# A 12-stage perceiver kernel on one core: weights of three late stages loaded two stages earlier, and a new order of TensorE's work between the scores of the rotary attention

## The chip, the cores and the metric

The kernel runs on one core of a Trainium2 chip. The metric is the device time of one execution in microseconds (us); lower is better. All values are float32.

## The reference

A residual `x` (16 batches of 64 latents, 128 features) goes through four layers of three blocks. Each block reads the layer-normed residual and adds its result to it. The last six are the ones that matter here:

```python
x = x + L2_xattn(ln(x), ctx, ctx, ...)   # single-head attention to 1601 context rows a batch
x = x + L2_attn(ln(x), ...)              # x+g1*(ln(x)@proj_w.T+proj_b), then an MLP of width 512
x = x + L2_ffn(ln(x), ...)               # mixture of 8 experts, the best 2
x = x + L3_xattn(ctx, ln(x), ...)        # 8 heads of 64, context keys with rotary positions
x = x + L3_attn(ln(x), ...)              # 16 heads of 8, latent attention:
    q_lat = (x @ Wq_down).reshape(b, t, 16, 64)
    q_c, q_e = q_lat @ Wq_up_c, q_lat @ Wq_up_e       # k in the same way, v = v_lat @ Wv_up
x = x + L3_ffn(ln(x), ...)               # gated recurrence over 32 steps:
    f = sigmoid(x_t @ wf.T + c @ uf.T + bf)           # i and g in the same way, with wi, ui, wc, uc
    c = f * c + i * g
```

## The kernel before, in words

The residual stays in SBUF as `lat` [128, 8, 128]. The 12 blocks are 12 stages, one after the other. A stage owns its SBUF and PSUM tensors and its semaphores; each has a program for every engine (SP issues all DMAs, PE, ACT, DVE, POOL), written out by hand, and its order is that of the code. When a stage ends, its semaphores are cleared and all engines meet at a barrier (L51 to L54). So no work of one stage lies beside another's, and each stage begins by loading its weights.

**L2_xattn** (`single_head_stage`, L1726). Work goes by pairs of batches. SP loads the context of a pair into `staged` (L1799 to L1803) when the pair before has left it; PE turns (transposes) it (L1867), makes the scores (L1879), turns the probabilities (L1890) and sums (L1903). Pairs 0, 1 and 2 are issued first, the rest in a loop.

**L2_attn** (`projected_mlp_stage`, L3006). SP issues 14 loads: three weights (`proj_rows`, `fc1_rows`, `fc2_rows`, 576 KB) and eleven small ones. PE waits for all of them (L3056), turns the weights in nine transposes (L3059 to L3062), turns the first half of the normalised tokens `z` (L2503) and multiplies by the projection (L3067). DVE makes the second `z` out of it, PE turns that too, and then come the matmuls of fc1 (L3076). ACT takes the square roots of both layer norms (L148), copies the turned weights out of PSUM (L3102 to L3104) and then the turned `z` (L2516).

**L3_xattn** (`rotary_attention_stage`, L1076). 16 batches (8 pairs, parity 0 and 1), each with four tiles t = 0 to 3 of two heads each, so 64 tiles. For a tile PE makes the scores of two heads against 1665 keys (L1290, eight matmuls of 512 columns and two short ones), ACT the exponentials and their scaling by the row sums (L1479). Behind the scores follow four slots j = 0 to 3. In each, PE turns a quarter of the probabilities of the tile before (`turn_probs`, L1302; the last slot has two short transposes), makes a quarter of the next tile's keys (`project`, L1278 to L1280), does one or two tiles of the sums (L1316) and, in some slots (`BETWEEN`, L1102), a "between": in t = 1 and 2 it turns four tiles of the next batch's context (L1258) at j = 1 and 2 (1) or j = 1 and 2 (2); in t = 0 of odd batches it makes the next pair's queries at j = 1 (L1265); in t = 3 of even ones the output at j = 2. `turn_probs` and the between share one PSUM bank, `bank_a`, which ACT must empty into SBUF before PE fills it again: L1486 for the probabilities, L1451 for the context, L1457 for the queries, which L1461 then places with four copies. The keys go on over DVE (L1665, L1667) and POOL (L1600), which makes `projected`, the input of the next scores.

**L3_attn** (`latent_attention_stage`, L3186). SP issues three loads of 512 KB (`down`), ten of 1 to 2 KB (`up`) and five more. PE turns `down` in 24 transposes (L3266), multiplies it by `up` (L3274, 24 products of 24 or 16 columns), so that up and down projection are folded into `heads` and `headsV`, turns the normalised residual `y` (L2503), and multiplies (L3284). `y` comes from DVE (L139).

**L3_ffn** (`gated_recurrence_stage`, L3479). SP issues eight loads of 64 KB (`rows`, the gate weights) and five small ones (`bias`). PE waits for all 13, turns the eight weights (L3523), turns `y` (L2503) and multiplies (L3535); 16 steps follow one after the other.

## Time and profile before

| | |
|---|---|
| median of 3 runs | 2897.18 us (2894.28 to 2900.27) |
| the profiled execution, its own time | 2901.51 us |
| its span in the trace | 2899.4 us |
| busy: PE, DVE, ACT, POOL | 2575.8, 1792.9, 1632.2, 1403.3 us |
| mean granted TensorE clock | 0.93 of full speed |
| L2_xattn, from about 1628 to 1754 | 126 us |
| L2_attn, to 1817 | 63 us |
| L3_xattn with its start, 1945 to 2722 | 777 us |
| L3_attn, to 2832 | 110 us |
| L3_ffn, to 2899 | 67 us |

The profiled execution took 4.33 us longer than the median. Times in the trace count from the start of the span. Busy PE time is the time in which matmuls are under way, not work at full rate.

### The profile page before, as it was taken

How to read it: one execution, taken by the hardware profiler on the slowest of the kernel's cores; microseconds unless marked ns; L12 is line 12 of the kernel's file. 1: busy time of each engine (PE TensorE's matmuls, PEld its weight loads, DVE VectorE, ACT ScalarE, POOL GpSimd, SP SyncE). 2: the span in 40 equal slices, each digit the busy share in tenths (PEclk: the TensorE clock that was granted, in tenths of full speed). 3: DMA queues.
4: the chain of work that ended last, by engine and by line, in shares of the span. 5: the costliest groups of instructions: out<-in, count | busy, mean ns of one | idle time of the engine just before them, and what ended most of it. 6: DMA issues, size and time to landing. Idle time of an engine off the chain costs nothing. (4 is left out here: it accounts for less than half of the span.)

```text
span 2899.4 us, 43919 instructions
## 1 busy us (share of the span) xinstructions
PE 2575.8 (89%) x16307; PEld 2149.0 (74%) x16307; DVE 1792.9 (62%) x3737; ACT 1632.2 (56%) x2861; POOL 1403.3 (48%) x1112
## 2 busy tenths in 40 slices
PE   5999998687999999999958795878999999999767
PEld 4899988476999999999957564775666676666546
DVE  7888874545555555545535446437888888888262
ACT  4888884335666666666623343325666666665332
POOL 1787774112666666666600260206566665665040
PEclk9999999788999999999978897888999999999775
DMA  3323321013111111110001240211000000000000
GB/s 109 104 75 99 105 59 36 14 30 87 35 35 35 35 29 41 29 42 24 12 8 42 72 114 16 59 32 58 13 24 13 24 21 16 24 13 1 25 1 15
DMA packets 222574, 117.83 MB, mean 41 GB/s; under 512 B 21368, under 2 KB 217632, under 8 KB 222368
## 3 DMA queue, kind: packets, MB, share of 16 engines
q1 hardware_dynamic: 222368, 115.11, 14.4%
q8 instruction: 127, 2.08, 0.3%
q14 instruction: 79, 0.65, 0.1%
HBM read 100.39 MB, written 13.64 MB: 39 GB/s over the span
## 5 line engine op out<-in xcount | busy, mean ns | idle before, releaser
L846 POOL TENSOR_TENSOR L_xattn_held<-L_xattn_held,L_xattn_shift 128x512 f32<-128x512 f32 (+1 forms) x613 | 762.8, 1290 | 296.5 <-ACT L_xattn_shift L766 296.4
L564 PEld LDWEIGHTS L_xattn_acc<-L_xattn_rows,L_xattn_held 128*128 128x128 f32 (+2 forms) x5120 | 618.4, 192 | 34.8 <-DVE L_xattn_mixed L949 9.2
L564 PE MATMUL L_xattn_acc<-L_xattn_rows,L_xattn_held 128*128 128x129 f32 (+2 forms) x5120 | 627.9, 275 | 5.6 <-DVE L_xattn_mixed L949 5.6
L970 DVE TENSOR_TENSOR L_xattn_running<-L_xattn_ring,L_xattn_running 128x512 f32<-128x512 f32 (+1 forms) x384 | 264.2, 688 | 268.7 <-PE L_xattn_ring L546 257.0
L1600 POOL TENSOR_TENSOR L_xattn_projected<-L_xattn_along,L_xattn_crossed 128x512 f32<-128x512 f32 (+1 forms) x256 | 271.6, 1072 | 280.9 <-DVE L_xattn_crossed L1667 279.1
L756 ACT ACTIVATE L_xattn_held<-L_xattn_held 128x512 f32<-128x512 f32 (+2 forms) x640 | 400.4, 631 | 0.2
L749 ACT COPY L_xattn_held<-L_xattn_ring 128x512 f32<-128x512 f32 (+1 forms) x416 | 243.3, 585 | 227.9 <-DVE L_xattn_running L970 193.3
L544 PE MATMUL L_xattn_ring<-L_xattn_queries_hi,L_xattn_keys_hi 128*128 128x512 f32 (+2 forms) x640 | 281.7, 440 | 3.4 <-DVE L_xattn_keys_lo L874 2.0
L546 PE MATMUL L_xattn_ring<-L_xattn_queries_hi,L_xattn_keys_lo 128*128 128x512 f32 (+2 forms) x640 | 254.0, 397 | 0.0
L545 PE MATMUL L_xattn_ring<-L_xattn_queries_lo,L_xattn_keys_hi 128*128 128x512 f32 (+2 forms) x640 | 253.6, 396 | 0.0
L1316 PE MATMUL L_xattn_sums<-L_xattn_probT,L_xattn_rows 128*128 128x256 f32 (+2 forms) x896 | 249.7, 386 | 0.6 <-ACT L_xattn_mixed L1492 0.6
L1486 ACT COPY L_xattn_probT<-L_xattn_bank_a 128x512 f32<-128x512 f32 (+2 forms) x320 | 138.9, 454 | 175.3 <-PE L_xattn_bank_a L1302 173.9
L1290 PE MATMUL L_xattn_score<-L_xattn_projected,L_xattn_queries 128*128 128x512 f32 (+1 forms) x512 | 199.6, 526 | 8.8 <-POOL L_xattn_projected L1600 8.3
L747 ACT ACTIVATE L_xattn_held<-L_xattn_ring,L_xattn_mask_now 128x512 f32<-128x512 f32 (+1 forms) x224 | 153.3, 684 | 74.8 <-DVE L_xattn_running L966 59.3
L1665 DVE TENSOR_TENSOR L_xattn_along<-L_xattn_bank_p,L_xattn_rot_cos 128x512 f32<-128x512 f32 (+1 forms) x256 | 151.6, 592 | 49.5 <-PE L_xattn_bank_p L1280 45.2
L1290 PEld LDWEIGHTS L_xattn_score<-L_xattn_projected,L_xattn_queries 128*128 128x128 f32 x512 | 95.7, 193 | 115.1 <-issue 56.5
L1316 PEld LDWEIGHTS L_xattn_sums<-L_xattn_probT,L_xattn_rows 128*128 128x128 f32 (+2 forms) x896 | 160.8, 192 | 24.8 <-issue 0.9
L966 DVE SCALAR_TENSOR_TENSOR L_xattn_running<-L_xattn_ring,L_xattn_mask_now,L_xattn_running 128x512 f32<-128x512 f32 (+2 forms) x208 | 154.6, 743 | 29.1 <-PE L_xattn_ring L546 26.2
L1302 PE MATMUL L_xattn_bank_a<-all_ident,L_xattn_prob 128*128 128x128 f32 (+2 forms) x896 | 145.4, 279 | 29.2 <-ACT L_xattn_turned L1451 14.9
L1675 DVE TENSOR_REDUCE L_xattn_peak<-L_xattn_score 128x1 f32<-128x1024 f32 (+1 forms) x128 | 127.1, 1021 | 64.6 <-PE L_xattn_score L1290 63.3
L1302 PEld LDWEIGHTS L_xattn_bank_a<-all_ident,L_xattn_prob 128*128 128x128 f32 (+2 forms) x896 | 103.0, 142 | 72.4 <-ACT L_xattn_turned L1451 36.8
L1667 DVE TENSOR_TENSOR L_xattn_crossed<-L_xattn_bank_p,L_xattn_rot_sin 64x512 f32<-64x512 f32 (+1 forms) x256 | 152.1, 594 | 3.5
(575 smaller groups left out, 4866.6 us busy)
## 6 DMA issues: line engine op xcount, KB each, us to landing
L_xattn_raw<-in_ctx SPq DMA_DIRECT2D x16, 768.0 KB
context_normalised<-L_xattn_fresh SPq DMA_DIRECT2D x16, 768.0 KB
L_xattn_rows<-context_normalised SPq DMA_DIRECT2D x16, 768.0 KB
L_xattn_fresh<-in_ctx SPq DMA_DIRECT2D x16, 768.0 KB
L_xattn_rows<-in_ctx SPq DMA_DIRECT2D x16, 768.0 KB
L_xattn_staged<-in_ctx SPq DMA_DIRECT2D x16, 768.0 KB
L_xattn_xhat<-context_normalised SPq DMA_DIRECT2D x16, 768.0 KB
L_ffn_w<-in_L_ffn_W SPq DMA_DIRECT2D x2, 896.0 KB, 5.4
```

The lines of the kernel that those rows point to most:

```text
L544: nc.tensor.matmul(bank, hi, q_hi, start=True, stop=False)
L545: nc.tensor.matmul(bank, hi, q_lo, start=False, stop=False)
L546: nc.tensor.matmul(bank, lo, q_hi, start=False, stop=True).then_inc(tile_done, 1)
L564: mm = nc.tensor.matmul(acc[:, c // 2, c % 2 * WIDE:(c % 2 + 1) * WIDE], held[0:n, u % 2, k, c * P:(c + 1) * P], rows[0:n, b % 2, k, :], s ...
L749: kept = nc.scalar.copy(dst, bank)
L756: nc.scalar.activation(held[0:n, u % 2, k, :], held[0:n, u % 2, k, :], ACT.Exp, scale=scale).then_inc(prob_ready, 1)
L846: nc.gpsimd.tensor_tensor(tile, tile, shift[0:keys_of_tile[k]], ALU.subtract).then_inc(shifted, 1)
L970: seen = nc.vector.tensor_tensor(most, bank, most, ALU.max)
L1290: mm = nc.tensor.matmul(score[:, c0:c0 + n], queries[:, pair % 2, parity, t * P:(t + 1) * P], projected[:, t % 2, c0:c0 + n], start=True, ...
L1302: turn = nc.tensor.transpose(bank[0:n, i * P:(i + 1) * P], prob[:, t % 2, c0:c0 + n], core.ident[:])
L1316: mm = nc.tensor.matmul(sums[:, 0:GCOLS], rows[0:n, parity, k, :], probT[0:n, group, k, :], start=(k == 0), stop=(k == KT - 1))
L1600: nc.gpsimd.tensor_tensor(projected[:, t % 2, c0:c0 + n], along[:, c0:c0 + n], crossed[:, c0:c0 + n], ALU.add)\
```

## The change

1. A new class `Ahead` holds `heads`, `headsV` and `gate_wT` in SBUF until the program ends, and the rows of the weights while L2_xattn and L2_attn run. Its 24 loads (3 for the MLP, 3 `down`, 8 gate weights, 10 `up`; some 2.6 MB) are issued on SP in L2_xattn, behind the loads of pair 2 and ahead of those of pair 3. The MLP has 11 loads left, L3_attn 5 and L3_ffn 5. POOL's memset of `up` goes along.
2. In L2_attn PE waits for the three weights alone, turns them, then turns `down` (24 transposes) and the gate weights (8) through three banks, and makes the 24 products `heads` between the projection and the turn of the second `z`. ACT has the eight copies `keep_later` between its square roots, and the copies of `heads`. DVE has the four small operations on `up`.
3. L3_attn and L3_ffn lose these loads, transposes, copies and products.
4. In the rotary attention the sums lie in a slot according to `SPLIT`, and in the slot behind one with a between `project` comes ahead of `turn_probs`. On ACT the copies that place the queries and the rounding of the own keys move from the slot of the between to the next one, behind its copy of the probabilities.
5. There is one more clearing of semaphores with its barrier behind L2_attn, and one more at the program's end.

```diff
+    SPLIT = {0: ((2, 0), (1, 1), (2, 0), (1, 0)), 1: ((2, 0), (1, 1), (2, 0), (1, 0)),
+             2: ((2, 0), (1, 1), (2, 0), (1, 0)), 3: ((2, 0), (2, 0), (1, 1), (1, 0))}
...
+                        if projects and j - 1 in BETWEEN[t]:
+                            project(*following(pair, parity, t), j)
                         if turns:
                             turn_probs(*preceding(pair, parity, t), j)
-                        if projects:
+                        if projects and j - 1 not in BETWEEN[t]:
                             project(*following(pair, parity, t), j)
...
                         if turns:
                             keep_probs(preceding(pair, parity, t)[2], j)
+                        if BETWEEN[t].get(j - 1) == "queries" and not last:
+                            if parity == 1:
+                                place_queries(pair + 1)
+                            keep_own(*after)
...
             load_staged(1, 1)
             during(0, 0)
+            core.ahead.load(sp, weights(core.w, "L2_attn"), weights(core.w, "L3_attn"), weights(core.w, "L3_ffn"))
             with sp.Fori(0, (PAIRS - 2) // 2 - 1) as j:
...
+            pe.wait_ge(ahead.down_loaded, ahead.DOWN_LOADS)
+            pe.wait_ge(ahead.gate_loaded, ahead.GATE_LOADS)
+            for n, (kind, j) in enumerate(LATER):
+                if n >= 3:
+                    pe.wait_ge(later_kept, n - 2)
...
             turn_tiles_pe(nc, pe, core.ident[:], z[:], bank[0:2], z_ready, 1, z_turned, by_halves=True)
...
+        with ExitStack() as loading:
+            core.ahead = Ahead(nc, ctx, loading)
+            STAGES["L2_xattn"](core, w)
+            STAGES["L2_attn"](core, w)
```

PE in the rotary attention, a tile t = 1, from the first turn of context (L1258, after L1261) at j = 1 to the last slot. `prob` are the probabilities, `bank_p` the keys. Before:

```order
L1258 MATMUL L_xattn_bank_a<-all_ident,L_xattn_gained 128x128 x4
L1316 MATMUL L_xattn_sums<-L_xattn_probT,L_xattn_rows 128x256
L1302 MATMUL L_xattn_bank_a<-all_ident,L_xattn_prob 128x128 x4
L1278 MATMUL L_xattn_bank_p<-L_xattn_keys_hi,L_xattn_wk_hi 128x512
L1279 MATMUL L_xattn_bank_p<-L_xattn_keys_hi,L_xattn_wk_lo 128x512
L1280 MATMUL L_xattn_bank_p<-L_xattn_keys_lo,L_xattn_wk_hi 128x512
L1316 MATMUL L_xattn_sums<-L_xattn_probT,L_xattn_rows 128x256
L1258 MATMUL L_xattn_bank_a<-all_ident,L_xattn_gained 128x128 x4
L1316 MATMUL L_xattn_sums<-L_xattn_probT,L_xattn_rows 128x256
L1302 MATMUL L_xattn_bank_a<-all_ident,L_xattn_prob 65x128
```

And now:

```order
L1261 MATMUL L_xattn_bank_a<-all_ident,L_xattn_gained 128x128 x4
L1319 MATMUL L_xattn_sums<-L_xattn_probT,L_xattn_rows 128x256
L1281 MATMUL L_xattn_bank_p<-L_xattn_keys_hi,L_xattn_wk_hi 128x512
L1282 MATMUL L_xattn_bank_p<-L_xattn_keys_hi,L_xattn_wk_lo 128x512
L1283 MATMUL L_xattn_bank_p<-L_xattn_keys_lo,L_xattn_wk_hi 128x512
L1305 MATMUL L_xattn_bank_a<-all_ident,L_xattn_prob 128x128 x4
L1319 MATMUL L_xattn_sums<-L_xattn_probT,L_xattn_rows 128x256 x2
L1261 MATMUL L_xattn_bank_a<-all_ident,L_xattn_gained 128x128 x4
L1281 MATMUL L_xattn_bank_p<-L_xattn_keys_hi,L_xattn_wk_hi 128x130
L1282 MATMUL L_xattn_bank_p<-L_xattn_keys_hi,L_xattn_wk_lo 128x130
L1283 MATMUL L_xattn_bank_p<-L_xattn_keys_lo,L_xattn_wk_hi 128x130
L1305 MATMUL L_xattn_bank_a<-all_ident,L_xattn_prob 65x128
```

Between a turn of context and the turn of probabilities behind it there now lie one matmul of the sums and three of the keys (first place), or the three short ones of the keys and no sums (second place).

ACT in the rotary attention, a tile t = 0 of an odd batch, from the queries' bank on. Before:

```order
L1457 COPY L_xattn_asked<-L_xattn_bank_a 128x512
L1461 COPY L_xattn_queries<-L_xattn_asked 32x8x64 x4
L1442 CAST L_xattn_keys_hi<-L_xattn_yT 128x64
L1486 COPY L_xattn_probT<-L_xattn_bank_a 128x4x128
L1486 COPY L_xattn_probT<-L_xattn_bank_a 65x128
```

And now:

```order
L1463 COPY L_xattn_asked<-L_xattn_bank_a 128x512
L1495 COPY L_xattn_probT<-L_xattn_bank_a 128x4x128
L1470 COPY L_xattn_queries<-L_xattn_asked 32x8x64 x4
L1449 CAST L_xattn_keys_hi<-L_xattn_yT 128x64
L1495 COPY L_xattn_probT<-L_xattn_bank_a 65x128
```

The copy of the probabilities of slot 2 goes ahead of the four copies that place the queries.

ACT at the start of L2_attn. Before:

```order
L148 ACT_TABLE_LOAD
L148 ACTIVATE L_attn_stats<-L_attn_square,all_small 128x4 x4
L3102 COPY L_attn_fc1T<-L_attn_bank 128x512
L3103 COPY L_attn_fc2T<-L_attn_bank 128x512
L3104 COPY L_attn_projT<-L_attn_bank 128x128
L2516 ACTIVATE L_attn_zT<-L_attn_bank,L_attn_cols 128x512 x2
```

And now:

```order
L3144 COPY L_attn_projT<-L_attn_bank 128x128
L3145 COPY L_attn_fc1T<-L_attn_bank 128x512
L148 ACT_TABLE_LOAD
L148 ACTIVATE L_attn_stats<-L_attn_square,all_small 128x4 x2
L3147 COPY L_attn_fc2T<-L_attn_bank 128x512
L3141 COPY L_attn_downT<-L_attn_bank 128x512 x4
L148 ACTIVATE L_attn_stats<-L_attn_square,all_small 128x4 x2
L3141 COPY L_attn_downT<-L_attn_bank 128x512 x2
L3141 COPY ahead_gate_wT<-L_attn_bank 128x512 x2
L2530 ACTIVATE L_attn_zT<-L_attn_bank,L_attn_cols 128x512 x2
```

Two copies stand ahead of the first square root, and nine between it and the turned `z`.

## Rows read from the trace of the kernel before

**Rows 1.** Windows: the rotary loop, 4 us of L2_xattn, 4 us of L3_attn.

```profile
core 0: us, PE busy (x) PEld busy (x) DVE busy (x) ACT busy (x) POOL busy (x), PEclk, DMA share, GB/s
1990.00:2700.00 710.00, 673.54 (x3329) 484.58 (x3327) 582.22 (x989) 451.61 (x721) 429.81 (x351) 1.00 0.06 17
1656.00:1660.00 4.00, 4.00 (x19) 3.46 (x18) 0.92 (x2) 1.42 (x3) 1.44 (x1) 0.50 1.06 288
2732.00:2736.00 4.00, 3.04 (x21) 2.37 (x20) 0.47 (x4) 2.25 (x4) 0.00 (x0) 0.87 0.20 44
```

**Rows 2.** Timeline of L3_attn's start: start, us, engine, [idle before <- releaser].

```profile
2722.83 0.36 SPq L3243 DMA_DIRECT2D L_attn_down<-in_L_attn_Wq_down  x1
2727.16 1.11 DVE L139 TENSOR_SCALAR L_attn_y<-all_lat,L_attn_square,L_attn_stats 128x128 f32<-128x128 f32 x4
2729.37 4.25 PE L3266 MATMUL L_attn_bank<-all_ident,L_attn_down 128*128 128x128 f32 x20 [8.72 <-DMA L_attn_down<-in_L_attn_Wv_down]
2730.80 0.59 SPq L3251 DMA_DIRECT2D L_attn_wc<-in_L_attn_Wc  x1
2735.23 9.30 PE L3274 MATMUL L_attn_bank<-L_attn_up,L_attn_downT 128*128 128x24 f32 x48 [0.77 <-ACT L_attn_downT L3366]
2746.99 5.20 PE L3284 MATMUL L_attn_bank<-L_attn_heads,L_attn_yT 128*128 128x384 f32 x10 [0.68 <-ACT L_attn_yT L2514]
```

**Rows 3.** Timeline of L3_ffn's start.

```profile
2836.03 0.43 SPq L3517 DMA_DIRECT2D L_ffn_bias<-in_L_ffn_bf  x1
2836.54 1.11 DVE L139 TENSOR_SCALAR L_ffn_y<-all_lat,L_ffn_square,L_ffn_stats 128x128 f32<-128x128 f32 x4
2840.04 1.97 PE L3523 MATMUL L_ffn_bank<-all_ident,L_ffn_rows 128*128 128x128 f32 x8 [9.90 <-DMA L_ffn_bias<-in_L_ffn_in_c]
2844.49 2.79 PE L3535 MATMUL L_ffn_bank<-L_ffn_yT,L_ffn_wT 128*128 128x64 f32 x12 [0.77 <-ACT L_ffn_yT L2514]
```

**Rows 4.** Waits of the rotary stage (us idle, times, longest); then its timeline, a tile t = 1.

```profile
PEld L_xattn_bank_a L1302 <- ACT L_xattn_turned L1451: 36.8, 60, 1.0
...
2356.76 0.66 PE L1302 MATMUL L_xattn_bank_a<-all_ident,L_xattn_prob 128*128 128x128 f32 x4 [0.30 <-ACT L_xattn_turned L1451]
2357.17 0.48 PE L1278 MATMUL L_xattn_bank_p<-L_xattn_keys_hi,L_xattn_wk_hi 128*128 128x512 f32 x1
2360.75 2.96 PE L1290 MATMUL L_xattn_score<-L_xattn_projected,L_xattn_queries 128*128 128x512 f32 x8
```

**Rows 5.** Timeline: a tile t = 0 of an odd batch, from the queries' copies.

```profile
2391.87 2.50 ACT L1461 COPY L_xattn_queries<-L_xattn_asked 32x512 f32<-32x512 f32 x4
2395.18 0.43 PE L1302 MATMUL L_xattn_bank_a<-all_ident,L_xattn_prob 128*65 128x128 f32 x2 [1.12 <-ACT L_xattn_probT L1486]
2396.22 1.02 PE L1290 MATMUL L_xattn_score<-L_xattn_projected,L_xattn_queries 128*128 128x512 f32 x2
```

**Rows 6.** Timeline of L2_xattn: SP's loads and PE's turns of pair 3.

```profile
1655.95 2.86 SPq L1803 DMA_DIRECT2D L_xattn_staged<-in_ctx  x1
1666.43 0.40 SPq L1801 DMA_DIRECT2D L_xattn_staged<-in_ctx  x1
1676.45 1.09 PE L1867 MATMUL L_xattn_lane<-all_ident,L_xattn_staged 128*128 128x128 f32 x8
```

**Rows 7.** Timeline of L2_attn, and the first DMA of L2_ffn behind it.

```profile
1754.77 1.28 ACT L148 ACT_TABLE_LOAD   x1 [4.27 <-PEq L54]
1764.95 1.11 PE L3059 MATMUL L_attn_bank<-all_ident,L_attn_fc_rows 128*128 128x128 f32 x4 [12.29 <-DMA L_attn_cols<-in_L_attn_lnh_b]
1769.81 3.78 PE L3067 MATMUL L_attn_bank<-L_attn_projT,L_attn_zT 128*128 128x128 f32 x16 [0.97 <-ACT L_attn_zT L2516]
1780.15 1.11 PE L2503 MATMUL L_attn_bank<-all_ident,L_attn_z 128*128 128x128 f32 x4 [6.56 <-DVE L_attn_z L139]
1815.00 1.23 DVE L3183 TENSOR_TENSOR all_lat<-all_lat,L_attn_z 128x1024 f32<-128x1024 f32 x1
1816.98 0.34 SPq L2200 DMA_DIRECT2D L_ffn_w<-in_L_ffn_W  x1
```

More of the change, by code:

```diff
@@ L1303, in turn_probs, with sum_context @@
                 filled("A", turn)
-            def sum_context(pair, parity, group, part, piece, turned, tiles=slice(None)):
+            def sum_context(pair, parity, group, tiles, turned):
                 b = pair * 2 + parity
-                if part == 0 and piece == 0 and tiles.start is None:
+                if tiles.start == 0:
                     pe.wait_ge(a_free, turned)
@@ L1336, in batch @@
                     back, group, part = sums_of_slot(t)
+                    tile = part * HALF
                     for j in range(len(QUADS)):
+                        sums, between = not (first and back), BETWEEN[t].get(j)
+                        ahead, behind = SPLIT[t][j]
+                        if projects and j - 1 in BETWEEN[t]:
+                            project(*following(pair, parity, t), j)
                         if turns:
                             turn_probs(*preceding(pair, parity, t), j)
-                        if projects:
+                        if projects and j - 1 not in BETWEEN[t]:
                             project(*following(pair, parity, t), j)
@@ L1343, in batch @@
                             late(j)
-                        sums, between = not (first and back), BETWEEN[t].get(j)
                         if sums:
-                            sum_context(*(before if back else (pair, parity)), group, part, j, turned, slice(None, 1))
+                            sum_context(*(before if back else (pair, parity)), group, range(tile, tile + ahead), turned)
                         if between == "queries":
@@ L1355, in batch @@
                             turn_context(*after, between)
-                        if sums:
-                            sum_context(*(before if back else (pair, parity)), group, part, j, turned, slice(1, None))
+                        if sums and behind:
+                            sum_context(*(before if back else (pair, parity)), group, range(tile + ahead, tile + ahead + behind), turned)
+                        tile += ahead + behind
                     if t % 2 == 0:
@@ L1515, in batch @@
                             if parity == 1 and not last:
-                                keep_queries(pair + 1)
-                            if not last:
-                                keep_own(*after)
+                                take_queries()
                         elif between == "output":
@@ L1553, in _ @@
             keep_own(0, 0)
[L1554 removed]
+            take_queries()
+            place_queries(0)
             keep_rows(0, 0)
@@ L3069, in _ @@
             mm.then_inc(proj_done, 1)
+            pe.wait_ge(up_ready, 1)
+            pe.wait_ge(later_kept, len(LATER))
+            for n, (at, width) in enumerate(((0, 12), (192, 12), (384, 8))):
+                for pair in range(8):
+                    cols = slice(at + pair * 2 * width, at + (pair + 1) * 2 * width)
+                    mm = nc.tensor.matmul(bank[7][:, cols].rearrange("p (r c) -> p r c", r=2), downT[:, n, pair, :],
+                                          ahead.up[:, n, :, 0:width], start=True, stop=True)
+            mm.then_inc(heads_done, 1)
             turn_tiles_pe(nc, pe, core.ident[:], z[:], bank[0:2], z_ready, 3, z_turned, by_halves=True)
@@ L3130, in _ @@
             nc.vector.tensor_tensor(x[:], x[:], over_tiles(row["proj_b"][:], TILES), ALU.add)
+            dve.wait_ge(ahead.up_loaded, ahead.UP_LOADS)
+            for half in range(2):
+                own = ahead.up[half * SEQ:(half + 1) * SEQ, 0:2, half]
+                pairs = own[:, :, 4:8].rearrange("p n (a b) -> p n a b", b=2)
+                partner = own[:, :, 8:12].rearrange("p n (a b) -> p n a b", b=2)
+                nc.vector.tensor_scalar(partner[:, :, :, 0], pairs[:, :, :, 1], -1.0, None, ALU.mult)
+                last = nc.vector.tensor_copy(partner[:, :, :, 1], pairs[:, :, :, 0])
+            last.then_inc(up_ready, 1)
             dve.wait_ge(proj_done, 1)
```

172 lines of the change are left out of this document (77 added, 95 removed).

## The prediction

> **What bounds the kernel now.** I read the windows by stage first. The rotary loop is bound by PE: busy 673.54 of 710 us at the full clock, so PE is idle for 36.5 us of it, while DVE has 582 and POOL 430 [rows 1]. Nothing that only reorders this loop can win more than those 36.5 us. Then I read the timelines of the stage starts, where the reader is to see idle time in front of PE's first matmul: 8.72 us in L3_attn and 9.90 us in L3_ffn, both ended by a DMA [rows 2, 3], and 12.29 us in L2_attn, also ended by one [rows 7]. Last, the waits of the rotary stage: the weight loads of `turn_probs` wait 60 times for ACT's copy of the turned context, 36.8 us in all or 0.61 each [rows 4].
>
> The sum is made against the profiled execution, 2901.51 us, and is then taken off the median, 2897.18, which lies 4.3 lower.
>
> **L3_attn.** The first product is now held by `y` alone. DVE makes it from 2727.16 for 1.11 us, so it is there at 2728.3 [rows 2]. The turn of the second half (four transposes, at the pace of the eight in L3_ffn, 1.97 us, so 1.0 [rows 3]) ends at 2729.3, ACT's copy takes some 0.7, and PE starts another 0.7 behind it, as the wait of L3284 shows [rows 2]: 2730.7 instead of 2746.99, so 16.3 us less. What goes with it is also what warmed the clock: 0.87 in the stretch of the 24 transposes [rows 1]. The products of L3284 may run at half the clock for longer; their first ten take 5.20 us [rows 2]. I charge 0.7, with ends of 0 and 3. The five DMAs that are left were issued from 2730.80, at 0.59 us, and now start at 2722.8 [rows 2], so they are in before DVE and ACT ask for them. **-15.6** (-13 to -17).
>
> **L3_ffn.** `y` is ready at 2836.54 + 1.11 = 2837.65. One more us for the turn, 0.7 for the copy, 0.77 to the start [rows 3]: 2840.1 instead of 2844.49. The bias loads, issued until after 2836 behind the eight weights at 0.43 us each [rows 3], come 3 us earlier and are wanted by ACT behind the first product. The cover of the whole edit is the layer norm in front of `y`; were a bias late, it would take back 1 us. **-4.35** (-3.5 to -4.7).
>
> **Rotary, t = 1 and 2.** In the first place PE is idle 0.30 us between the context turn and `turn_probs`, and the weight load waits 0.61 on average [rows 4]; I take 0.47, the gap left when the two sums matmuls ahead of it run at their pace. Three key matmuls now fill it: they take 0.8 us, from 2357.17 to the next row's sums [rows 4]. So 0.47 goes. In the second place the filler was two sums matmuls and is now three short key matmuls, a little shorter, so that stall stays and grows by 0.08. Net 0.39 in t = 1 and, by the same count, 0.34 in t = 2. The next scores start at 2360.75 [rows 4] less this, since the keys come from POOL in time there. For 15 batches: 15 x 0.73 = 11.0 us.
>
> **Rotary, t = 0 of odd batches.** The four copies that place the queries hold ACT for 2.50 us; behind them stands the copy of the probabilities for which PE then waits 1.12 us, and behind that come the scores at 2396.22 [rows 5]. With the new order this wait, and some 0.6 us of smaller ones in the same slots, go: 1.7 us. But the copies now stand ahead of the last copy of the slot and of the scaling of the next probabilities, on the path to the next tile's first turn, which I work out as 1.0 us late. Left is 0.7 us for each of 7 tiles: 5.0 us. Together the rotary stage gives **-16** (-8, if half of the gaps reopen a slot later; -20, if the lateness is hidden).
>
> **L2_xattn.** SP is done with pair 2 at 1655.95 + 2.86 = 1658.8 and then idle until the loads of pair 3 at 1666.43 [rows 6]. Into this gap go 24 issues. L3_attn issues 13 of the same from 2722.83 to 2730.80, 7.97 us or 0.61 each [rows 2]; the other eleven at 0.43 [rows 3] are 4.7: together 12.7, until 1671.5 at least. The bytes, 2.6 MB, take 9.1 us at the 288 GB/s of this stretch, where the DMA engines are full [rows 1], so they end with the issues. Pair 3's loads start 5 to 6 us late and PE, which turns this pair at 1676.45 [rows 6], finds them landing at about 1679.4 (issued at 1672; a pair is 1.64 MB, 5.7 us at that rate, and I estimate 1.7 for start and completion). I take 3 us of waiting plus 1 for a clock that falls (it is 0.50 in the window at 1656, behind such a wait [rows 1]): **+4** (0, if the buffers have more slack than I see; +8, if the clock stays low for a pair).
>
> **L2_attn.** Without the three weights PE waits for `mlp_loaded` alone, which is long in: the nine transposes start at 1754 instead of 1764.95, and the 32 later ones run while the layer norm does. ACT now copies twice ahead of its table load (1.28 us, first thing at 1754.77 before [rows 7]), so the square root comes 2.2 us later, and the first `z` about 1 us; against this the wait for the last weight is gone. I put the projection at 1768.6 instead of 1769.81 [rows 7]: -1.2. Then the `heads` products stand in front of the second turn of `z`. L3_attn's 48 records took 9.30 us, mostly at half the clock [rows 2]; at the full clock it would be 5.6. They lie beside 6.56 us in which PE waited for DVE [rows 7]: between 1 us of slack and 2.7 us too long, and DVE has four small operations more. I take +1.2, nearer to the low end because the 32 transposes ahead of them warm the clock. Sum **0** (-1.5 to +3).
>
> The table load moves behind two copies. The trace has the square root directly behind it, as the projection's timeline starts: 1.28 us and no more [rows 7]. The Trainium skill, page "ScalarE: Activation LUTs", section "What ACT_TABLE_LOAD costs", puts a drain of about 1380 ns behind the load, 2.66 us in all. By it the moved load would make the first `z` 1.4 us later still, and the sum would be 1.4 us less of a gain; the row speaks against it.
>
> **Barriers.** From DVE's last operation, 1815.00 + 1.23, to the first DMA of the next stage are 0.75 us [rows 7]. One such clearing is added behind L2_attn and one barrier at the end: **+0.7** (0.2 to 1.5).
>
> **The sum.** -15.6 - 4.35 - 16 + 4 + 0 + 0.7 = -31.2: 2870.3 us for the profiled execution, 2866.0 for the median. All ends on one side give -42 and -10.5; likely they offset, so this case alone spans 2858 to 2874.
>
> **The rivals.** (1) *The rotary order gives little.* The stalls are short, and PE's queue could meet the same copy one slot later, or the keys made earlier do nothing because DVE (82% busy) sets the pace. For it: DVE's share; against it: PE has 95% and the wait is ended by ACT's copy, not by DVE. Then the rotary gives -4 instead of -16: 2878. (2) *The loads cost L2_xattn nearly nothing and the gaps close fully*: +1 and -20, so 2859. (3) *L2_xattn pays more*: the context falls behind for several pairs, since SP issues in order and its buffers come free late; each pair then starts late and the half clock doubles the price. +12 instead of +4: 2874. (4) *Slower.* The one mechanism that could do it stands in the rotary stage: `turn_probs` behind `project` delays ACT's copies, ACT's scaling of the next probabilities comes later, and each tile's first turn waits for it. All 60 tiles pay. To eat the 15 us that are left without the rotary gain it has to be over 0.25 us a tile; to make the kernel slower than before by 0.2%, 0.35 us. In the tile of [rows 4] about 1.3 us lie between the scaled probabilities and their first turn, so a delay of 0.4 us should be hidden. At 0.5 us a tile it would be 30 us: 2912. (5) *The change doesn't do what it says*: the loads may stand in front of a buffer wait and come late, so that L2_attn waits on them. Two stages, some 80 us, lie between, so this is next to nothing.
>
> **How the numbers follow.** My forecast (2858 to 2874) 55%, rival 1 16%, rival 2 10%, rival 3 14%, rival 4 with 5 and what I don't see 5%. The range goes from 2854 to 2881: it takes in rivals 1, 2 and 3 at their centres. Two tenths of a per cent, 5.8 us, is what a measurement of this kernel can tell from no change; faster by more than that means below 2891.4. Only rival 4, or several bad ends at once, comes above: faster 0.95, same 0.03, slower 0.02.
>
> **What would show it.** In the changed profile: PE's first product in L3_attn at 8 us behind the stage's start instead of 24, with no DMA wait before it; in L3_ffn 8 instead of 12; the waits of `turn_probs` on the copy of the context at half their sum or less, and PE's idle time in the rotary loop down from 36.5 us to near 20; a wait of some 3 us for a DMA on pair 3 in L2_xattn; the second turn of `z` in L2_attn still ended by DVE. I am wrong if the rotary loop is not shorter by at least 8 us, if a pair behind the fourth still waits for its context, or if the `heads` products end the wait of the second `z`.

## The result and the profile after

The changed kernel takes 2863.78 us in the median (2858.3 to 2867.22, 4 runs) against 2898.72 us before (2894.28 to 2902.74, 4 runs): a ratio of 0.9878, with a 95% interval of 0.9856 to 0.99. The profiled execution took 2862.94 us, with a span of 2861.0.

Cut at the first instruction of each stage, the two traces give this account (us; the first six stages are the same code, and the first of them alone was 3.8 us shorter in this execution):

| stage | before | after | difference | forecast |
|---|---|---|---|---|
| L0 to L1, six stages | 1623.8 | 1620.0 | -3.8 | 0 |
| L2_xattn | 124.61 | 131.20 | +6.6 | +4 |
| L2_attn, with one more clearing | 62.23 | 65.61 | +3.4 | 0, and 0.7 for both barriers |
| L2_ffn | 127.91 | 128.39 | +0.5 | 0 |
| L3_xattn | 777.93 | 754.14 | -23.8 | -16 |
| L3_attn | 109.51 | 92.20 | -17.3 | -15.6 |
| L3_ffn to the end, with one more barrier | 66.97 | 62.93 | -4.0 | -4.35 |

Without the first six stages the sum is -34.7; forecast were -31.2. The total is near, but single terms were off by several us, in both directions: the rotary stage gave 7.8 us more than forecast, L2_xattn and L2_attn cost 2.6 and 2.9 us more.

**L3_attn and L3_ffn**, from the changed kernel's timeline (start, us, engine, what it waited for):

```profile
2705.84 0.36 SPq L3290 DMA_DIRECT2D L_attn_wc<-in_L_attn_Wc  x1
2710.06 1.11 DVE L139 TENSOR_SCALAR L_attn_y<-all_lat,L_attn_square,L_attn_stats 128x128 f32<-128x128 f32 x4
2711.23 1.11 PE L2517 MATMUL L_attn_bank<-all_ident,L_attn_y 128*128 128x128 f32 x4 [0.16 <-DVE L_attn_y L139]
2713.01 8.61 PE L3305 MATMUL L_attn_bank<-ahead_heads,L_attn_yT 128*128 128x384 f32 x16 [0.68 <-ACT L_attn_yT L2528]
...
2798.04 0.33 SPq L3515 DMA_DIRECT2D L_ffn_bias<-in_L_ffn_bf  x1
2805.02 2.82 PE L3528 MATMUL L_ffn_bank<-L_ffn_yT,ahead_gate_wT 128*128 128x64 f32 x12 [0.68 <-ACT L_ffn_yT L2528]
```

The first product starts 7.2 us behind L3_attn's first DMA where it was 24.2 [rows 2], and 7.0 us behind L3_ffn's first DMA. What it waits for is DVE's `y` and ACT's copy of it, no DMA.

**L2_xattn**, the same view, the end of the new loads on SP and PE at pair 3; then windows (us, busy times of PE, PEld, DVE, ACT and POOL, granted clock, DMA share, GB/s):

```profile
1667.79 0.60 SPq L3623 DMA_DIRECT2D ahead_rows_up<-in_L_attn_Wv_up  x1
1669.14 0.40 SPq L1813 DMA_DIRECT2D L_xattn_staged<-in_ctx  x1
1677.77 1.77 PE L1880 MATMUL L_xattn_lane<-all_ident,L_xattn_staged 128*128 128x128 f32 x8 [5.17 <-DMA L_xattn_staged<-in_ctx]
1679.47 2.47 PE L1916 MATMUL L_xattn_sums<-L_xattn_rows,L_xattn_probT 128*64 128x128 f32 x24
```

```profile
1662.00:1664.00 2.00, 2.00 (x31) 1.71 (x29) 0.77 (x3) 1.86 (x3) 0.24 (x1) 1.00 1.05 364
1664.00:1666.00 2.00, 2.00 (x31) 1.83 (x28) 0.89 (x2) 0.26 (x2) 0.00 (x0) 1.00 0.70 147
1666.00:1668.00 2.00, 1.65 (x14) 1.35 (x13) 0.92 (x2) 1.26 (x3) 0.14 (x1) 1.00 0.06 1
1678.00:1680.00 2.00, 2.00 (x14) 1.67 (x14) 0.42 (x1) 1.28 (x2) 0.00 (x0) 0.50 1.12 320
```

PE waits 5.17 us for pair 3's context. The traffic of the weights is over by 1666 (from 364 and 147 GB/s it falls to 1), while SP goes on issuing small loads until 1668.4. No later pair waits for its context. And the clock, at its higher level (2.4 GHz) up to 1678, is at half behind the wait: the eight turns take 1.77 us instead of 1.09 [rows 6].

**L2_attn**, PE's timeline:

```profile
1757.74 0.63 PE L3075 MATMUL L_attn_bank<-all_ident,ahead_rows_fc_rows 128*128 128x128 f32 x4 [2.14 <-PEq L54]
1771.56 3.79 PE L3093 MATMUL L_attn_bank<-L_attn_projT,L_attn_zT 128*128 128x128 f32 x16 [0.87 <-ACT L_attn_zT L2530]
1775.13 10.26 PE L3102 MATMUL L_attn_bank<-ahead_rows_up,L_attn_downT 128*128 128x24 f32 x48
1785.23 1.95 PE L2517 MATMUL L_attn_bank<-all_ident,L_attn_z 128*128 128x128 f32 x8
1788.05 10.11 PE L3113 MATMUL L_attn_bank<-L_attn_fc1T,L_attn_zT 128*128 128x512 f32 x16 [0.87 <-ACT L_attn_zT L2530]
```

The projection starts 13.9 us behind the stage's start, before it was 15.0 [rows 7]. But from there to the turn of the second `z` it is 13.67 us instead of 10.34, and no wait for DVE stands in that row any more: PE comes straight from the `heads` products, which took 10.26 us.

**The rotary stage**, waits (us idle, times, longest):

```profile
PEld L_xattn_bank_a L1305 <- ACT L_xattn_turned L1458: 12.4, 33, 0.6
PE L_xattn_bank_a L1305 <- ACT L_xattn_turned L1458: 6.6, 15, 0.4
```

The first row was 36.8 us in 60 waits [rows 4]. Part of it came back one step later, at the turn of the context, whose weight loads wait for ACT's copy of the probabilities. Before and after:

```profile
PEld L_xattn_bank_a L1258 <- ACT L_xattn_probT L1486: 6.8, 16, 1.5
PEld L_xattn_bank_a L1261 <- ACT L_xattn_probT L1495: 14.2, 45, 1.5
```

Over the same part of the loop, with its length now 685.2 us instead of 710:

```profile
1996.80:2682.00 685.20, 660.90 (x3323) 488.48 (x3321) 581.47 (x989) 450.34 (x721) 429.59 (x351) 1.00 0.06 17
```

PE is idle for 24.3 us instead of 36.5 [rows 1]. So only 12.2 of the 24.8 us came out of PE's idle time, and 12.6 out of time in which it counted as busy.

### The profile page after: what moved, and what is told of

The parts are those of the page before. It is cut to its first block and busy times, and to the rows that moved or that the text cites. A ratio compares the mean times of both kernels' runs of the same rounds, so it can differ in the third digit from the quotient of the medians.

```text
span 2861.0 us, 43942 instructions
## 1 busy us (share of the span) xinstructions
PE 2563.2 (90%) x16307; PEld 2152.8 (75%) x16307; DVE 1789.2 (63%) x3737; ACT 1631.0 (57%) x2861; POOL 1403.2 (49%) x1112
## 5 line engine op out<-in xcount | busy, mean ns | idle before, releaser
L564 PEld LDWEIGHTS L_xattn_acc<-L_xattn_rows,L_xattn_held 128*128 128x128 f32 (+2 forms) x5120 | 618.5, 192 | 34.7 <-DVE L_xattn_mixed L949 9.1
L1319 PE MATMUL L_xattn_sums<-L_xattn_probT,L_xattn_rows 128*128 128x256 f32 (+2 forms) x896 | 243.6, 383 | 0.6 <-ACT L_xattn_mixed L1501 0.6
L1293 PEld LDWEIGHTS L_xattn_score<-L_xattn_projected,L_xattn_queries 128*128 128x128 f32 x512 | 96.1, 191 | 112.6 <-issue 65.8
L1305 PE MATMUL L_xattn_bank_a<-all_ident,L_xattn_prob 128*128 128x128 f32 (+2 forms) x896 | 143.3, 277 | 16.7 <-ACT L_xattn_prob L1488 6.9
L1679 DVE TENSOR_TENSOR L_xattn_crossed<-L_xattn_bank_p,L_xattn_rot_sin 64x512 f32<-64x512 f32 (+1 forms) x256 | 152.0, 594 | 3.5
L1678 DVE TENSOR_TENSOR L_xattn_crossed<-L_xattn_bank_p,L_xattn_rot_sin 64x512 f32<-64x512 f32 (+1 forms) x256 | 149.6, 584 | 3.4
```

The lines of the kernel that those rows point to most:

```text
L564: mm = nc.tensor.matmul(acc[:, c // 2, c % 2 * WIDE:(c % 2 + 1) * WIDE], held[0:n, u % 2, k, c * P:(c + 1) * P], rows[0:n, b % 2, k, :], s ...
L1293: mm = nc.tensor.matmul(score[:, c0:c0 + n], queries[:, pair % 2, parity, t * P:(t + 1) * P], projected[:, t % 2, c0:c0 + n], start=True, ...
L1319: mm = nc.tensor.matmul(sums[:, 0:GCOLS], rows[0:n, parity, k, :], probT[0:n, group, k, :], start=(k == 0), stop=(k == KT - 1))
```

## The experiments

Stage lengths in the table are cut in each kernel's trace as above. The rotary periods are the time from one tile's first score to the next one's, for batches 1 to 14.

| kernel | L2_xattn | L2_attn | L3_xattn | L3_attn | L3_ffn | median us |
|---|---|---|---|---|---|---|
| before | 124.61 | 62.23 | 777.93 | 109.51 | 66.97 | 2898.72 |
| after | 131.20 | 65.61 | 754.14 | 92.20 | 62.93 | 2863.78 |
| rotary order only | 124.39 | 62.46 | 754.32 | 105.64 | 67.04 | 2870.13 |
| loads ahead only | 131.18 | 65.70 | 778.01 | 94.05 | 62.21 | 2888.99 |
| all loads last | 123.74 | 61.79 | 753.90 | 92.00 | 62.89 | 2855.05 (one run) |
| small loads last | 124.67 | 65.53 | 754.11 | 92.12 | 62.93 | 2861.26 (one run) |
| heads last | 131.05 | 66.77 | 754.01 | 91.28 | 62.96 | 2863.08 (one run) |
| PE's order only | 132.01 | 60.25 | 766.73 | 92.57 | 63.08 | 2870.63 (one run) |
| ACT's order only | 130.64 | 60.01 | 771.70 | 91.35 | 62.87 | 2876.35 (one run) |
| placing behind the scaling | 131.04 | 63.42 | 754.06 | 89.97 | 63.55 | 2858.57 (one run) |
| placing spread | 131.14 | 65.71 | 751.09 | 91.36 | 63.15 | 2861.24 (one run) |
| heads split | 130.98 | 62.86 | 754.50 | 91.15 | 63.08 | 2864.15 (one run) |
| the three together | 123.95 | 62.89 | 751.35 | 91.16 | 63.05 | 2849.76 |
| after, once more | 131.07 | 65.75 | 754.53 | 92.15 | 62.92 | 2866.45 |

The first stage, untouched in all of them, takes 503.3 to 507.7 us, and L1_xattn 821.2 to 825.4; a single run's total says less than its stages.

**The two halves apart.** Each half was put alone into the kernel before.

> The kernel before with the new rotary order alone. If the two halves of the change are independent, the rotary stage is 23 to 24 us shorter than before, as in the changed kernel, no other stage moves by more than 0.3 us, and the time is near 2874. If the rotary stage gained because of what is loaded ahead (fewer DMAs beside it, another layout in SBUF), its own gain is under 20 us.

> The changed kernel with the rotary stage of before. Sum of the stage lengths seen in the changed kernel: +6.6 in L2_xattn, +3.4 in L2_attn, -17.3 in L3_attn, -4.0 in L3_ffn, so about -11 us: near 2887. The rotary stage keeps its 777.9 us. If the rotary gain came partly from the loads ahead, that stage is shorter here by the missing part.

Measured: the order alone gives a ratio of 0.9901 (0.9874 to 0.9928), the loads ahead alone 0.9959 (0.9942 to 0.9975). The rotary stage takes 754.32 and 778.01 us, as with and without its order in the two kernels, so the halves are independent there. One length moved that was not expected to: L3_attn is 3.9 us shorter in the kernel with the order alone, though its code is that of before. Most of it is the clock. In that kernel the `heads` products ran at 0.82 of the full clock, in the one before at 0.56, and took 2.8 us less than the 9.30 of [rows 2]:

```profile
2707.63 6.54 PE L3286 MATMUL L_attn_bank<-L_attn_up,L_attn_downT 128*128 128x24 f32 x48 [0.77 <-ACT L_attn_downT L3378]
```

So a stage length of these tables carries up to some us of clock. Behind its first product L3_attn takes 82.8 to 86.9 us in the kernels that have the weights ahead.

**What L2_xattn pays for.** The call `core.ahead.load(...)` moved, whole or for its ten small loads:

```diff
             during(0, 0)
-            core.ahead.load(sp, ...)
             with sp.Fori(0, (PAIRS - 2) // 2 - 1) as j:
                 during(2 * j + 1, 1)
                 during(2 * j + 2, 0)
             during(PAIRS - 3, 1)
+            core.ahead.load(sp, ...)
```

> The changed kernel with all 24 loads behind the last context load of L2_xattn instead of ahead of pair 3's. Theory: the 6.6 us of L2_xattn come only from pair 3's context being issued late; then the stage is back at 124.6 to 125 us, and L2_attn starts without a DMA wait, since 30 us are left. Rival: the loads cost bandwidth wherever they stand, or the clock falls for another reason; then at least 3 us stay. Or they land too late and L2_attn waits for them: over 1 us in front of its first transpose.

> The changed kernel with only the ten small loads (up, 1 to 2 KB each, some 14 KB in all) behind the last context load; the fourteen large ones (2.6 MB) stay ahead of pair 3. Theory, issue time: the ten took SP 6.4 us, so pair 3 is issued 6.4 us earlier, just where it was before, and its wait of 5.2 us shrinks to 0 to 2 us (the bytes ahead of it were all in 3.9 us before its issue). Rival, bytes: the 2.6 MB ahead of it hold it as before, and the wait stays at 4 us or more, since ten loads of 14 KB weigh nothing.

The timeline of the kernel with the ten small loads last (SP and PE at pair 3):

```profile
1667.07 0.40 SPq L1813 DMA_DIRECT2D L_xattn_staged<-in_ctx  x1
1677.93 1.09 PE L1881 MATMUL L_xattn_lane<-all_ident,L_xattn_staged 128*128 128x128 f32 x8 [0.52 <-DMA L_xattn_staged<-in_ctx]
```

Here the 2.6 MB still stand ahead of pair 3, but the wait is 0.52 us instead of 5.17, the eight turns take 1.09, and the stage is 124.67 us long. So it was SP's time to issue ten more loads, not the bytes, that cost 6.5 us. Before the change SP was idle for 7.6 us between the loads of pair 2 and pair 3 [rows 6]; the fourteen large loads take it 6.8 us and fit in, all 24 take 13.6 and do not. That the ten left over were the small ones is the order of this program; the large ones behind the small ones were not tried. The bytes were not free either: in this kernel pair 3 needs 10.9 us from its first issue to PE's turns, with the wait of 0.52 at its end, where the changed kernel needs 8.6. They took up slack that was there. With all 24 behind the last context load the wait is gone and the stage takes 123.74 us; L2_attn's first transpose comes right at its start, so nothing is late.

**What L2_attn pays for.** First the `heads` products were moved behind the fc1 matmuls.

```diff
-            (24 products)
             turn_tiles_pe(nc, pe, core.ident[:], z[:], bank[0:2], z_ready, 3, z_turned, by_halves=True)
             pe.wait_ge(zT_kept, 4)
             for t in range(TILES):
                 ... fc1 ...
+            pe.wait_ge(hid_biased, TILES)
+            (24 products)
```

> The changed kernel with the 24 heads products behind the fc1 matmuls of L2_attn, where PE waits 7.2 us for DVE, instead of ahead of the second turn of z; ACT's copies of them at the stage's end. Theory: the products (10.26 us at half the clock) cost L2_attn 3 us, by reaching 2.1 us past the second z and by holding up its first half; then the stage is 62.5 to 63 us instead of 65.6. Rival: the 3.4 us come from the later square root, the eight copies on ACT and the added barrier; then the stage stays above 64.5. At half the clock the products would also reach past the 7.2 us, which would cost up to 3 us again there.

Measured: 66.77 us, 1.2 longer than after. The timeline of this kernel shows the gap closed in one place and opened in the other:

```profile
1781.77 1.12 PE L2517 MATMUL L_attn_bank<-all_ident,L_attn_z 128*128 128x128 f32 x4 [6.54 <-DVE L_attn_z L139]
1797.31 10.14 PE L3111 MATMUL L_attn_bank<-ahead_rows_up,L_attn_downT 128*128 128x24 f32 x48 [2.31 <-issue]
1807.29 1.95 PE L3121 MATMUL L_attn_bank<-all_ident,L_attn_hid 128*128 128x128 f32 x8
```

The second `z` is on time again, 3.3 us earlier in the stage than in the changed kernel. But the products run at half the clock there too (0.51), begin 2.31 us behind the fc1 matmuls (by the edit they wait until the last bank is free; the row names no releaser), and from the start of fc1 to the turn of `hid` it is 22.3 us instead of 17.3: 5.0 more, against the 3.3 won. The expectation had named this price, up to 3 us, only as a remark; it was the outcome.

Then the products were split: the eight of q while PE waits for ACT's copies, sixteen in the old place, in `bank[4]`, and the four operations on `up` on POOL instead of DVE.

```diff
             for n, (kind, j) in enumerate(LATER):
+                if n == 7:
+                    pe.wait_ge(up_ready, 1)
+                    pe.wait_ge(later_kept, 2)
+                    fold(0)
...
+            fold(1)
+            fold(2).then_inc(heads_done, 1)
```

> The changed kernel with the eight heads products of q done while PE waits for ACT's copies, ahead of the last group of turned weights, the other sixteen where all were, and the small operations on up on POOL. Theory: in front of the second z stand 16 products of 0.43 us at half the clock, 6.9 us, which just fit beside DVE's 6.6 us; so L2_attn is 62 to 63 us also where the clock is low, instead of 65.6, and 60 or below where it is high. Rival: the products ahead of the first z delay it by as much as they save behind: 65 us and more at the low clock.

PE's timeline of this kernel:

```profile
1769.40 3.45 PE L3086 MATMUL L_attn_bank<-ahead_rows_up,L_attn_downT 128*128 128x24 f32 x16
1779.93 6.85 PE L3086 MATMUL L_attn_bank<-ahead_rows_up,L_attn_downT 128*128 128x24 f32 x32
1786.68 1.12 PE L2517 MATMUL L_attn_bank<-all_ident,L_attn_z 128*128 128x128 f32 x4
1787.96 1.12 PE L2517 MATMUL L_attn_bank<-all_ident,L_attn_z 128*128 128x128 f32 x4 [0.17 <-DVE L_attn_z L139]
```

The stage takes 62.86 us, 2.7 less. The second `z` is turned 24.7 us behind the stage's start instead of 27.5; its second half is waited for again, and the sixteen products just fit in, at the low clock. That 2.8 is at the same clock of 0.50 during the products in both kernels, so it is the split's. The stage's total carries more than that: with the products not split and at 0.50 too, the kernel with the placing behind the scaling came to 63.42, because its fc1 matmuls met a higher clock (8.52 us instead of 10.11).

**Which of the two orders gives what in the rotary stage.** In the changed kernel, once ACT and once PE got its order of before.

> The changed kernel with ACT's order of before in the rotary stage (the queries placed at once), PE's order new. By the prediction's split PE's order gives 11.0 of 16 us; measured are 23.8 for both. If the split holds in proportion, the stage is at 777.9 - 16 = 762 us (after: 754.1). If ACT's order does nothing by itself, it stays at 754 to 755.

> The changed kernel with PE's order of before in the rotary stage and ACT's new. By the prediction 5.0 of 16 us come from the 7 tiles t = 0 of odd batches: the stage at 770 to 773 us, t = 0 of odd batches 1.0 to 1.7 us shorter (12.67 before), t = 1 of odd batches up to 1.0 longer (11.90 before), all others as before. If the two orders need each other, both single runs together give clearly less than 23.8.

Periods in us (even / odd batches; left out are t = 0 of batch 1, which is 0.7 to 0.9 us longer than the other odd ones, and three tiles with a clock at half, told below):

| tile | before | PE's order | ACT's order | both |
|---|---|---|---|---|
| t = 0 | 10.47 / 12.67 | 10.55 / 12.67 | 10.47 / 11.35 | 10.55 / 10.91 |
| t = 1 | 12.55 / 11.90 | 12.14 / 11.51 | 12.54 / 12.09 | 12.12 / 12.24 |
| t = 2 | 11.09 | 10.70 | 11.09 | 10.70 |
| t = 3 | 11.72 / 9.82 | 11.49 / 9.73 | 11.71 / 9.82 | 11.49 / 9.74 |

PE's order alone makes the stage 11.2 us shorter, ACT's alone 6.2, both 23.8. The missing 6.4 us are mostly in tiles that had a clock at half. With PE's order alone three odd batches had t = 1 at 13.2 instead of 11.51. PE's timeline there, and the window of it, beside a window of the kernel before in batch 0:

```profile
2207.02 0.43 PE L1305 MATMUL L_xattn_bank_a<-all_ident,L_xattn_prob 128*65 128x128 f32 x2 [1.56 <-ACT L_xattn_probT L1495]
2208.08 4.64 PE L1293 MATMUL L_xattn_score<-L_xattn_projected,L_xattn_queries 128*128 128x512 f32 x8
2221.27 2.96 PE L1293 MATMUL L_xattn_score<-L_xattn_projected,L_xattn_queries 128*128 128x512 f32 x8
```

```profile
2208.00:2211.50 3.50, 3.50 (x7) 1.41 (x6) 0.65 (x3) 1.76 (x2) 0.46 (x1) 0.51 0.02 5
```

```profile
2004.00:2008.00 4.00, 3.64 (x10) 2.10 (x9) 2.95 (x6) 2.47 (x5) 1.79 (x3) 0.50 0.00 0
```

The scores take 4.64 us instead of 2.96. Before them PE had been idle for 1.56 us in one place and was at 0.51 of its clock right after. That happens in three of the seven odd batches, 5.0 us in all; the other four have the same wait of 1.57 us and keep the full clock, so the wait alone doesn't decide it. In the kernel with ACT's order alone the clock was at half twice in the later part of batch 0, which came out 2.9 us longer than before. Over batches 1 to 14, with the three falls taken off, the two orders give 12.8 and 8.0 us, together 20.8, and both at once give 20.1: they add up there. The rest of the 23.8 is mostly batch 0, which takes 48.1 us before and 44.9 now. Its last two tiles (t = 2 and 3) were at 0.86 and 0.84 of the clock, the window of batch 0 above lies in them, and are at 1.00 now. This is no accident of one trace: batch 0 takes 48.1 us in both kernels with both old orders (before, loads ahead only), 51.1 with ACT's order alone, and 44.9 to 45.6 in all those with PE's new order. How much of the 3.2 us is the clock and how much the order itself is not shown.

**What holds t = 1 of odd batches at 12.24.** The prediction blamed the four copies that place the queries, on the way to the scaled probabilities. They were moved behind the scaling:

```diff
                     normalise(pair, parity, t)
+                    if t == 0 and parity == 1 and not last:
+                        place_queries(pair + 1)
```

> The changed kernel with the four copies that place the queries (2.5 us on ACT) moved on, behind the scaling of the probabilities of tile t = 0, where ACT waits about 3 us for PE. The prediction said that these copies delay the next tile's first turn: t = 1 of odd batches went from 11.90 to 12.25. If that is so, it is back at 11.9 or below and t = 0 stays at 10.9: the stage 2 to 4 us shorter than 754.1. Rival: the copies now delay the exponentials of t = 1, and the stage is no shorter or longer.

The stage stayed as it was, 754.06 us and t = 1 at 12.23, as the expectation's rival had it. ACT's timeline of this kernel shows where the 2.50 us went:

```profile
2206.75 1.69 ACT L1488 ACTIVATE L_xattn_prob<-L_xattn_prob,L_xattn_rinv 128x1665 f32<-128x1665 f32 x1
2208.51 2.50 ACT L1470 COPY L_xattn_queries<-L_xattn_asked 32x512 f32<-32x512 f32 x4
2211.30 0.59 ACT L1495 COPY L_xattn_probT<-L_xattn_bank_a 128x512 f32<-128x512 f32 x1
```

The scaling comes in time, but now the first copy of the probabilities in t = 1 is late, 4.3 us behind the tile's start, where it is at 3.4 in the odd batches of the kernel with PE's order alone, and the exponentials behind it are 0.7 us late too. Then the copies were taken apart, one in each of four slots of t = 2 and t = 3:

```diff
+            PLACE_AT = [(2, 3), (3, 1), (3, 2), (3, 3)]
...
+                        if parity == 1 and not last and (t, j) in PLACE_AT:
+                            place_queries(pair + 1, [PLACE_AT.index((t, j))])
```

> The changed kernel with the four copies that place the queries one by one in slots of the tiles t = 2 (slot 3) and t = 3 (slots 1 to 3) of odd batches, where ACT has gaps. Theory: the 2.5 us in one piece are what holds t = 1 of odd batches at 12.24 (the copies moved behind the scaling held its first copy of the probabilities instead, 4.31 us behind the start instead of 3.44). Then t = 1 of odd batches is at 11.5 to 11.6, as in most batches with PE's order alone, t = 2 and 3 grow by at most 0.3, and the stage is 3 to 5 us shorter than 754.1. Rival: t = 1 is held by something else (the context's copies); it stays at 12.2.

The rows of PE's scores in this kernel, an odd batch from t = 0 on:

```profile
2200.04 2.96 PE L1293 MATMUL L_xattn_score<-L_xattn_projected,L_xattn_queries 128*128 128x512 f32 x8
2210.96 2.97 PE L1293 MATMUL L_xattn_score<-L_xattn_projected,L_xattn_queries 128*128 128x512 f32 x8
2222.47 2.96 PE L1293 MATMUL L_xattn_score<-L_xattn_projected,L_xattn_queries 128*128 128x512 f32 x8
2233.16 2.97 PE L1293 MATMUL L_xattn_score<-L_xattn_projected,L_xattn_queries 128*128 128x512 f32 x8
2243.83 3.04 PE L1293 MATMUL L_xattn_score<-L_xattn_projected,L_xattn_queries 128*128 128x512 f32 x8 [0.77 <-issue]
```

t = 1 is at 11.51 as expected, and t = 0 of even batches fell from 10.55 to 9.88, which nobody had expected. But t = 3 of odd batches grew from 9.74 to 10.66, three times the 0.3 that was allowed. The stage gained 3.05 us, at the low end. So the copies did hold t = 1; in the three places that were tried they took part of the gain back elsewhere. Why t = 0 of even batches fell is open.

**The best version.** All loads last, the split products and the spread copies, with the changed kernel beside it on the same chip.

> The three together: all 24 loads behind the last context load, the spread placing and the split heads. Sum of what each should give against the changed kernel: 7.4 + 4 + 2 to 3, so 13 to 14 us less, near 2849. If the stages are independent the lengths are 124 (L2_xattn), 60 to 63 (L2_attn), 750 (L3_xattn).

> The changed kernel unchanged, beside the combined one, for a common measure: 2860 to 2867. The code of L2_attn was the same in six runs and the stage took 60.0 to 65.7 us; if the clock at the heads products is what differs (6.1 us at the high clock, 10.3 at the low), this run shows one of these lengths together with the matching duration of the products.

Together they take 2849.76 us (2847.88 to 2854.3, 5 runs), a ratio of 0.9817 (0.9803 to 0.983) to the kernel before; the changed kernel on the same chip took 2866.45 (2862.23 to 2868.91, 4 runs), 0.9878 (0.9863 to 0.9893). So 16.7 us more, of which the stages show 7.1 (L2_xattn), 2.9 (L2_attn), 3.2 (L3_xattn) and 1.0 (L3_attn); the two untouched attentions, L0 and L1, were longer in this profile. Whether the split products add anything here is open: with all loads last and the products whole, L2_attn took 61.79 us, less than the 62.89 of this kernel, at a clock of 0.74 during the products instead of 0.50.

## Why the prediction was right, and where it was off

- *L3_attn, -15.6.* Measured -17.3. `y` was ready and copied as the prediction had it, but it counted 0.7 us for ACT's copy and another 0.7 for the wait, which are the same thing: the row says 0.68 for both. The first product starts 17.0 us earlier instead of 16.3. The charge of 0.7 for the clock came, at 0.6: the sixteen products of `heads` take 8.61 us where they took 8.01 (the row of [rows 2] and its second part below), with a clock of 0.50 and 0.74 in the first two stretches of 4 us instead of 0.61 and 1.00. It was made up further on, where the scores of this stage took 5.35 us instead of 6.14 at a higher clock (0.66 over those 20 us instead of 0.59); nothing in the forecast had that. Had the trace of before met the clock of the kernel with the rotary order alone, the difference would be 13.4. So the -17.3, just outside the stated -13 to -17, is not good to better than some us.

```profile
2752.61 2.39 PE L3284 MATMUL L_attn_bank<-L_attn_heads,L_attn_yT 128*128 128x384 f32 x6 [0.41 <-ACT L_attn_qk L3374]
```

- *L3_ffn, -4.35.* The same double count: the first product starts 5.2 us earlier. The stage is only 4.0 shorter. The added barrier is 0.24 of the rest; from the first product to DVE's last operation it is 50.9 us instead of 50.1, with the clock of the last 27 us at 0.57 instead of 0.59.
- *Rotary, -16.* Measured -23.8, outside its own range of -8 to -20. The mechanism was right: the waits on the copy of the context went from 36.8 to 12.4 us, although 7.4 reopened at the turn of the context, as the lower end had feared. PE's part was forecast at 11.0 and gave 11.2 when alone, but by luck: over batches 1 to 14 it is 12.8 without the clock's three falls, these took 5.0 back, and batch 0 gave 3.1 that nobody had counted. t = 1 and t = 2 fell by 0.42 and 0.39 where 0.39 and 0.34 had been forecast. Missed was t = 3: there, too, `project` now goes ahead of `turn_probs`, behind the output, which gives 0.23 in even and 0.08 in odd batches, 2.2 us in all. Against it t = 0 of even batches is 0.08 longer, 0.6 us in all. ACT's part was 5.0 and gave 8: the lateness of t = 1 was worked out as 1.0 us against its gain, and was 0.74 (12.24 against 11.51). The path was not only the one named. The copies hold up whatever of ACT's work stands behind them, the scaling in one place, the first copy of the probabilities in the other. Batch 0 is the other part that was missed (3.2 us). And the bound that the prediction started from, PE's 36.5 us of idle time, is none: half of the gain came out of time that counts as busy.
- *L2_xattn, +4.* Measured +6.6: 5.17 us of waiting, where the term had 3, and 1.6 of a slower clock in the two rows behind it, where it had 1. PE was ready for the pair when it had been before (46.1 us behind the stage's start, 46.3 before); the term was mis-sized at its two others. Pair 3 was issued 6.4 us later than before as seen from the stage's start, where 5 to 6 had been forecast and 5.6 used, and its 1.64 MB took 8.6 us from the first issue to the start of the turns, not 7.4. Of these 7.4, the 1.7 for start and completion came from no row. The prediction also held issue and bytes to end together; they did not. The traffic ended some 2 us before the last issue, and the issue alone decided.
- *L2_attn, 0 (-1.5 to +3).* Measured +3.4, of which 0.5 is the added clearing (1.22 us between DVE's last operation and the next stage's first DMA, 0.75 before). The start was as forecast, -1.2. The step that failed is the cover of the `heads` products: +1.2 with the argument that the transposes warm the clock, +3.3 in fact. The 32 transposes come with 4.6 us of waiting for ACT, the clock was at 0.50 when the products began, and they took 10.26 us, above the upper bound of 9.30 that the forecast had from L3_attn's row. And +1.2 is not near the low end of its own bounds, as it says, but just above their middle (-1 to +2.7). The other 0.8 of the 3.4 stand behind the second `z`: fc1 took 10.11 us instead of 9.16.
- *Barriers, +0.7.* 0.47 and 0.24.
- *The ends.* The prediction adds them up to -42 and -10.5; its own terms give -43.0 and -12.0. Nothing hangs on it.
- *The table load.* ACT's copy ahead of the load and its first square root behind it, from the changed kernel:

```profile
1759.12 0.59 ACT L3145 COPY L_attn_fc1T<-L_attn_bank 128x512 f32<-128x512 f32 x1
1759.71 1.28 ACT L148 ACT_TABLE_LOAD   x1
1761.01 0.49 ACT L148 ACTIVATE L_attn_stats<-L_attn_square,all_small 128x4 f32<-128x4 f32 x2
```

There are 0.02 us between the load and the square root, and none ahead of it. The Trainium skill, page "ScalarE: Activation LUTs", section "What ACT_TABLE_LOAD costs", adds a drain of about 1380 ns to the load's 1283 ns; this trace shows none on either side, and the prediction was right to go by the row.

The prediction named three signs of being wrong. Two did not come: the rotary loop is shorter by far more than 8 us, and no pair behind the fourth waits for its context. The third did: the `heads` products, not DVE, end the wait of the second `z` in L2_attn. That part of the mechanism was wrong, and it cost 3.3 us instead of 1.2. Of the signs of being right, PE's idle time in the loop is 24.3 us (near 20 was forecast), the first products start at 7.2 and 7.0 us (8 and 8), and the waits of `turn_probs` are at a third (half or less).

Of the rivals none came about. The second had larger gaps closed and the loads hidden: the first half of it held, the second did not. The gains were 7.8 us (rotary) and 1.7 us (L3_attn) larger than forecast, the losses 2.6 us (L2_xattn) and 2.9 us (L2_attn) larger, and they partly cancelled. The difference was 34.9 us where 31.2 had been forecast, and the median of the kernel before came out 1.5 us higher with its fourth run; that the total is only 2.2 us off is partly luck and says little about its terms.

## What to carry to other kernels

When loads are pulled ahead, count the issues of the queue and not only the bytes: a gap of 7.6 us in SP's work held fourteen issues (2.6 MB), and the next ten (14 KB) pushed the context load behind them back by 6.4 us. Put them where the queue has nothing more to issue for a while, which here was free. Work pushed into another stage's gap has to be priced at both levels of the clock, since the same products took 6.1 to 10.3 us here; and a block of copies on an engine should be cut up before it is moved, since moved whole it holds up the next thing in line.

## What the runs showed of the hardware that was not expected

The code of L2_attn was the same in nine of the runs above (all but the two with the old stage, the one with heads last and the two with split products), and the stage took 60.0 to 65.8 us. The granted clock during the `heads` products accounts for much of it: 0.82 and 0.87 in the two shortest, 0.74 in the next (61.79), 0.50 in the other six, of which one is at 63.42 because of the clock in fc1. A window of the changed kernel and one of the kernel with PE's order alone, each at the start of these products:

```profile
1773.70:1777.70 4.00, 4.00 (x21) 4.00 (x21) 2.25 (x3) 0.00 (x0) 0.00 (x0) 0.50 0.00 0
```

```profile
1773.67:1777.67 4.00, 4.00 (x38) 4.00 (x37) 3.78 (x12) 0.02 (x1) 0.00 (x0) 1.00 0.00 0
```

The same instructions with the same code ahead of them ran at 1.2 GHz in one and at 2.4 GHz in the other, 21 records against 38 in 4 us, and the 48 records took 10.26 and 6.14 us. These two kernels are the same in all their code up to the end of L2_attn (they differ in the rotary stage, which comes later), and in both the clock was at its higher level in the 12 us ahead of the stage. The chip doesn't decide it either: two of the kernels measured on one chip had the products at 0.87 and 0.82, another there had 0.50. The split products make the stage less open to this in principle, but they were seen at the low clock alone. What decides which level such a stretch gets was not tested. A change of a few us in a stage like this, read from one execution of each kernel, can be the clock alone.
